# A six-layer local-attention network on one core: the order of every engine's work around the Gelu is rewritten

## The chip, the core and the metric

The kernel runs on one core of a Trainium2 chip. The time is device microseconds of one execution. Before the change the median of three runs is 1857.39 us (1855.83 to 1862.92).

## The reference, cut to what matters

```python
for i in range(6):                                   # DEPTH; x is (8, 256, 128), f32
    x = attn_layer(shift_tokens(x), Wqkv[i], q_scale[i], k_scale[i], Wo[i]) + x
    x = ffn_layer(shift_tokens(x), ln_g[i], ln_b[i], W1[i], b1[i], W2[i], b2[i]) + x

def attn_layer(x, Wqkv, qs, ksc, Wo):                # 16 heads of 64, windows of 32 keys
    q, k, v = split(x @ Wqkv)
    q, k = l2norm(q) * qs, l2norm(k) * ksc           # per token and head
    q, k = q * cos * scale + rotate_half(q) * sin * scale, ...
    sim = where(mask, -max, 8 * q @ k2.T)            # own window and the one before it
    return softmax(sim) @ v2 @ Wo

def ffn_layer(x, g, bln, W1, b1, W2, b2):
    xn = (x - mean) / sqrt(var + 1e-5) * g + bln
    a, gate = split(xn @ W1 + b1)                    # 341 each
    return a * gelu(gate) @ W2 + b2
```

Ahead of the layers come a LayerNorm and a linear attention, and behind them a SiLU gate. The change doesn't touch these.

## The kernel before, in words

The eight batch rows of 256 tokens go through the six layers as 48 steps (`STEPS`), one row and one layer each. A step's work is cut into four units `j` = 0 to 3: an octet of eight heads (`j // 2`) of one tile of 128 tokens (`j % 2`). Each engine has one program, written by hand as a `body(n)` with four slots `j`; steps 3 to 47, 45 of them, run in a hardware loop. In slot `j` of step `n`, with `u = 4n + j`, an engine works on several units at once: the projections and the rotation of unit `u`, the turn (transposition) and the scores of unit `u-2`, the values of unit `u-3`, and pieces of the feed-forward part of steps `n-2` and `n-3`. Every engine runs its own instructions in the order written, and semaphores tie them together.

What the names in the rows are, slot by slot:

- TensorE (PE): `project` writes `ps_q`, `ps_k`, `ps_v`; `turn_qk` writes `ps_qs` and `ps_tk`, and waits for `less_max` of the slot before (`sub_done`), since `ps_qs` held those scores; `turn_p` writes `ps_po`; `scores` needs ScalarE's copies `q_t` and `k_t`; `values` needs ScalarE's copy `p_bd`. `ps_a` is the output projection and the LayerNorm's mean and variance; `ps_f` is shared by `ln_spread`, the three `ff_up` parts and `ff_down`.
- VectorE (DVE): `rotate` (L1076 and L1078, for q and then k), `sum_squares` (L1084, `ssq`), `clamp` (L1094, `ssq_c`), `find_max` (L1116), `less_max` (L1121), `sums` (L1127 and the reciprocal `row_inv`, L1130), and three Newton steps of the inverse norm, `rn_a` (L1099), `rn_b` (L1105) and `rnorm` (L1111). The Newton steps read two tensors in SBUF each, on 128x18 elements. `rotate` of the next slot stands behind all of these.
- ScalarE (ACT): copies out of PSUM (L838), squares (L844), `start_norms` (a logarithm, L876, and an exponential, L878, of 128x18), the softmax's exponential (L944), `ff_copy` (L899, L901) and `gelu` (L906). The Gelu needs another table of functions, and a table load comes ahead of it and one behind it.
- GpSimd (POOL): `divide` (L433, needs `row_inv`), `add_halves` (L418, q and k), `normalise` (L426, q and k, needs `rnorm`), `ff_gate` (L440, L442) in slot 1, `split_slice` (L403, L406) in slot 2, where the layer isn't the last, and `round_x` (L450, L453) in slot 3. Its queue is in the order written as well.

The Gelu of a step stands at the end of ScalarE's slot 0, and its table is changed back in slot 1.

Of the kernel before, what the change touches and what calls it, by code (L numbers as in the profile page):

```python
# [33 lines left out]
QK_SCALE = 8.0  # L34
# [28 lines left out]
def build(nc, x, wq, wk, wv, wp, bp, conv_w, conv_b, wqkv, q_scale, k_scale, wo, ln_g, ln_b, w1, b1, w2,  # L63
          rotary, masks, eye, head_block, out):
    with ExitStack() as ctx:
# [305 lines left out]
        def _(pool):  # L371
# [116 lines left out]
        def _(pe):  # L488
# [281 lines left out]
        def _(act):  # L770
# [83 lines left out]
            def keep_turned(u, j, s):  # L854

                octet, tile = j // 2, j % 2
                wait(act, s_done, u - 1)
                act.wait_ge(tq_done, u + 1)
                copy(q_t[:, s, :], ps_qs[:]).then_inc(q_turned, 1)
                act.wait_ge(tk_done, u + 1)  # L860
# [42 lines left out]

            def gelu(m):
# [13 lines left out]
            def body(n):  # L918
                for j in range(UNITS):
                    u = UNITS * n + j  # L920
                    if live(u - 2):
                        keep_turned(u - 2, (j - 2) % UNITS, j % 2)
                    if live(u):
                        squares_of(u, 0, j % 2)
                    if j == 0 and live(u - 3):
                        keep_p(u - 3, (j - 3) % 2)
                    if live(u):
                        squares_of(u, 1, j % 2)
                    if j > 0 and live(u - 3):
                        keep_p(u - 3, (j - 3) % 2)  # L930
                    if j == 0 and live_batch(n - 2):
                        ln_square(n - 2)
                    if j == 1 and live_batch(n - 3):

                        nc.scalar.preload_act_table_set("natural_log_exp_and_others")
                    if normed(n, j):
                        start_norms(n, j)
                    if j == 0 and live_batch(n - 3):
                        ff_copy(n - 3, 2)
                    if j >= 2 and live_batch(n - 2):  # L940
                        ff_copy(n - 2, j - 2)
                    if live(u - 2):
                        act.wait_ge(sub_done, u - 1)
                        nc.scalar.activation(prob[:, j % 2, :], prob[:, j % 2, :], ACT.Exp,  # L944
                                             scale=QK_SCALE).then_inc(exp_done, 1)
                    if live(u):
                        keep_v(u, n, j)
                    if live(u - 3):
# [357 lines left out]
```

## Time and profile before

| | |
|---|---|
| median of three runs | 1857.39 us |
| profiled execution, own time | 1855.56 us |
| its span | 1853.8 us |
| TensorE busy | 1663.1 us, 90% |
| VectorE, ScalarE, GpSimd busy | 77%, 73%, 70% |
| one steady step | 35.70 us, of which TensorE 33.14 busy |

A busy share is taken over the whole span. TensorE's records are pipelined and their ends are modelled, so starts tell more than ends. In the timelines a row is one or several merged instructions: start in us, time in us, engine, line, operation, output and inputs, and in brackets the idle time of the engine ahead of it with what ended it. The next instruction of VectorE or ScalarE often starts a little before the recorded end of the one ahead.

### The profile page before, as it was taken

How to read it: one execution, taken by the hardware profiler on the slowest of the kernel's cores; microseconds unless marked ns; L12 is line 12 of the kernel's file. 1: busy time of each engine (PE TensorE's matmuls, PEld its weight loads, DVE VectorE, ACT ScalarE, POOL GpSimd, SP SyncE). 2: the span in 40 equal slices, each digit the busy share in tenths (PEclk: the TensorE clock that was granted, in tenths of full speed). 3: DMA queues.
4: the chain of work that ended last, by engine and by line, in shares of the span. 5: the costliest groups of instructions: out<-in, count | busy, mean ns of one | idle time of the engine just before them, and what ended most of it. 6: DMA issues, size and time to landing. Idle time of an engine off the chain costs nothing.

```text
span 1853.8 us, 68588 instructions
## 1 busy us (share of the span) xinstructions
PE 1663.1 (90%) x25968; PEld 1291.5 (70%) x26160; DVE 1430.3 (77%) x3041; ACT 1344.7 (73%) x2656; POOL 1293.3 (70%) x1283
## 2 busy tenths in 40 slices
PE   7889999999999999999999999999999999999973
PEld 5667777777777777677777777767777776777751
DVE  4588878878778787887778778788777777778755
ACT  4267777777777777777777777777777777777753
POOL 5287777777777777777777777777777777677720
PEclk9799999999999999999999999999999999999995
DMA  5011111111101011110111101111110111101000
GB/s 164 11 38 34 32 33 32 30 40 48 32 28 34 28 41 46 33 30 28 34 45 41 34 28 30 31 47 37 33 34 29 33 37 32 30 24 30 25 14 20
DMA packets 41406, 66.13 MB, mean 36 GB/s; under 512 B 7072, under 2 KB 16032, under 8 KB 41376
## 3 DMA queue, kind: packets, MB, share of 16 engines
q1 hardware_dynamic: 40224, 65.38, 11.7%
q10 hardware_dynamic: 1152, 0.34, 0.1%
q8 instruction: 20, 0.33, 0.1%
q14 instruction: 10, 0.08, 0.0%
HBM read 20.61 MB, written 1.05 MB: 12 GB/s over the span
## 4 chain that ended last, share of the span: by engine, by line
PE 68%; ACT 11%; issue 10%; DVE 9%; POOL 1%; ACTq 1%; DMA 0%; DVEq 0%
PE ps_a L490 11%; PE ps_f L490 11%; PE ps_qs L490 9%; PE ps_po L490 8%; PE ps_q L490 7%; PE ps_k L490 5%; PE ps_v L490 5%; PE ps_po L604 4%; PE ps_qs L596 3%; PE ps_tk L596 3%; ACT L906 2%; DVE ssq L1084 2%; DVE prob L1121 2%; ACT p_bd L838 2%; ACT squares L844 2%
## 5 line engine op out<-in xcount | busy, mean ns | idle before, releaser
L426 POOL TENSOR_TENSOR qk<-qk,rnorm 128x512 f32<-128x512 f32 x384 | 393.1, 1045 | 298.2 <-DVE rnorm L1111 298.2
L418 POOL TENSOR_TENSOR qk<-qk,qk_rot 128x512 f32<-128x512 f32 x384 | 483.7, 1276 | 111.1 <-DVE qk_rot L1078 110.8
L1084 DVE TENSOR_REDUCE ssq<-squares 128x8 f32<-128x512 f32 x384 | 257.6, 680 | 71.1 <-ACT squares L844 58.2
L490 PE MATMUL ps_qs<-k_t,q_t 64*32 64x64 f32 x12288 | 210.7, 218 | 67.6 <-ACT k_t L838 46.5
L838 ACT COPY p_bd<-ps_po 64x512 f32<-64x512 f32 x384 | 221.3, 576 | 34.7 <-PE ps_po L604 32.4
L433 POOL TENSOR_TENSOR prob<-prob,row_inv 128x512 f32<-128x512 f32 x192 | 200.3, 1043 | 51.5 <-DVE row_inv L1130 51.5
L1127 DVE TENSOR_REDUCE row_sum<-prob 128x8 f32<-128x512 f32 x192 | 131.7, 686 | 120.6 <-ACT prob L944 120.6
L490 PEld LDWEIGHTS ps_qs<-k_t,q_t 64*32 64x32 f32 x12288 | 179.7, 107 | 57.2 <-issue 57.2
L944 ACT ACTIVATE prob<-prob 128x512 f32<-128x512 f32 x192 | 121.2, 631 | 110.9 <-DVE prob L1121 107.6
L490 PEld LDWEIGHTS ps_po<-p_bd,v_back 128*64 128x64 f32 x3072 | 162.9, 137 | 49.5 <-issue 31.8
L490 PE MATMUL ps_po<-p_bd,v_back 128*64 128x64 f32 x3072 | 193.9, 225 | 1.6 <-ACT p_bd L838 1.5
L490 PE MATMUL ps_po<-p_bd,v_own 128*64 128x64 f32 x3072 | 189.5, 222 | 0.0
L490 PE MATMUL ps_a<-attn_t,wo_sb 128*64 128x257 f32 x1536 | 187.9, 386 | 0.0
L838 ACT COPY k_t<-ps_tk 128x512 f32<-128x512 f32 x192 | 112.9, 588 | 86.7 <-PE ps_tk L596 81.9
L490 PE MATMUL ps_f<-xn,w_sb 128*128 128x256 f32 (+1 forms) x576 | 160.6, 402 | 7.3 <-ACT ff_g L901 1.9
L1076 DVE TENSOR_TENSOR qk<-ps_q,table 128x512 f32<-128x512 f32 x192 | 132.6, 691 | 40.8 <-issue 29.6
L490 PEld LDWEIGHTS ps_po<-p_bd,v_own 128*64 128x64 f32 x3072 | 155.9, 138 | 0.0
L844 ACT ACTIVATE squares<-ps_k 128x512 f32<-128x512 f32 x192 | 115.2, 600 | 54.0 <-DVE qk_rot L1078 52.9
L1076 DVE TENSOR_TENSOR qk<-ps_k,table 128x512 f32<-128x512 f32 x192 | 131.0, 682 | 28.7 <-PE ps_tk L596 28.6
L604 PE MATMUL ps_po<-ident,prob 128*128 128x128 f32 x768 | 119.5, 278 | 31.0 <-POOL prob L433 31.0
L604 PEld LDWEIGHTS ps_po<-ident,prob 128*128 128x128 f32 x768 | 88.1, 140 | 82.5 <-issue 70.0
L844 ACT ACTIVATE squares<-ps_q 128x512 f32<-128x512 f32 x192 | 115.8, 603 | 40.8 <-DVE qk_rot L1078 40.7
(161 smaller groups left out, 4002.6 us busy)
## 6 DMA issues: line engine op xcount, KB each, us to landing
v_back<-v_own SPq DMA_DIRECT2D x192, 192.0 KB, 2.4
w_raw<-in_wqkv SPq DMA_DIRECT2D x48, 192.0 KB, 2.4
v_back<-v_own SPq DMA_DIRECT2D x96, 64.0 KB, 2.1
wo_sb<-in_wo SPq DMA_DIRECT2D x12, 256.0 KB, 3.0
w_sb<-in_w SPq DMA_DIRECT2D x6, 341.0 KB, 3.4
w_sb<-in_w SPq DMA_DIRECT2D x6, 192.0 KB, 2.7
x_in<-in_x SPq DMA_DIRECT2D x4, 256.0 KB, 5.0
out<-s_out SPq DMA_DIRECT2D x8, 128.0 KB, 1.9
```

The source lines that it names most:

```text
L418: nc.gpsimd.tensor_tensor(qk[:, s, i, :], qk[:, s, i, :], qk_rot[:, s, i, :], ALU.add).then_inc(added, 1)
L426: nc.gpsimd.tensor_tensor(heads(qk[:, s, i, :]), heads(qk[:, s, i, :]), rnorm[:, s, 8 * i:8 * i + 8].unsqueeze(2).to_broadcast([P, 8, HEAD ...
L433: nc.gpsimd.tensor_tensor(heads(prob[:, s, :]), heads(prob[:, s, :]), row_inv[:, s, :].unsqueeze(2).to_broadcast([P, 8, HEAD]), ALU.mult). ...
L490: return nc.tensor.matmul(o, lhs, rhs, start=start, stop=stop, **kw)
L596: last = nc.tensor.transpose(ps[:, P * c:P * c + P], qk[:, s, i, P * c:P * c + P], ident[:])
L604: last = nc.tensor.transpose(ps_po[:, P * c:P * c + P], prob[:, s, P * c:P * c + P], ident[:])
L838: return nc.scalar.copy(o, i)
L844: nc.scalar.activation(squares[:, s, OCTET * i:OCTET * i + OCTET], (ps_q, ps_k)[i][:], ACT.Square).then_inc((q_squared, k_squared)[i], 1)
L944: nc.scalar.activation(prob[:, j % 2, :], prob[:, j % 2, :], ACT.Exp, scale=QK_SCALE).then_inc(exp_done, 1)
L1076: V.tensor_tensor(heads(qk[:, s, i, :]), heads(ps[:]), cos.unsqueeze(1).to_broadcast([P, 8, HEAD]), ALU.mult)
L1084: V.tensor_reduce(ssq[:, s, 8 * i:8 * i + 8], heads(squares[:, s, OCTET * i:OCTET * i + OCTET]), AX, ALU.add).then_inc(ssq_done, 1)
L1127: V.tensor_reduce(row_sum[:, s, :], heads(prob[:, s, :]), AX, ALU.add).then_inc(sum_done, 1)
```

## The change: all four engines in another order

No operation is added or taken away; the matrix sizes and the tables stay.

- GpSimd: `normalise` is taken out of the end of its own unit's slot, and stands in the next slot, between `divide` and `add_halves`. `round_x` goes ahead of `add_halves` of slot 3.
- ScalarE: `keep_turned` becomes `keep_queries` and `keep_keys`; the attention copy, now of unit `u-4`, and the `ff_copy` parts stand between them. `gelu` and the last `ff_copy` go from slot 0 to slot 1, behind `keep_keys`. In slot 1, `start_norms` goes behind the exponential and `keep_v`.
- VectorE: in slot 1 `find_max` and `less_max` go ahead of `sum_squares`, and all Newton steps behind `sums`. In slot 2 `ln_normalise` goes behind `find_max`, and `after_ff` to just behind `rotate`.
- TensorE: `ln_spread` goes from early in slot 2 to behind that slot's scores, `ff_up` part 0 behind the values, and `ff_up` part 1 from early in slot 3 to behind `project` of v.

The diff, cut to its core:

```diff
 # GpSimd
                     if live(u - 3):
                         divide(u - 3, (j - 3) % 2)
+                    if live(u - 1):
+                        normalise(u - 1, (j - 1) % 2)
+                    if j == 3 and live(UNITS * (n + 1)):
+                        round_x(n + 1)
                     if live(u):
                         add_halves(u, j % 2)
...
-                    if j == 3 and live(UNITS * (n + 1)):
-                        round_x(n + 1)
-                    if live(u):
-                        normalise(u, j % 2)
 # TensorE
-                        if i == 0 and j == 2 and live_batch(n - 2):
-                            ln_spread(n, n - 2)
-                        if i == 0 and j == 3 and live_batch(n - 2):
-                            ff_up(n - 2, 1)
...
+                    if j == 3 and live_batch(n - 2):
+                        ff_up(n - 2, 1)
                     if live(u - 3):
                         turn_p(u - 3, (j - 3) % 2)
...
                     if j == 2 and live_batch(n - 2):
-                        ff_up(n - 2, 0)
+                        ln_spread(n, n - 2)
...
                     if live(u - 3):
                         values(u - 3, n if j >= 3 else n - 1, (j - 3) % UNITS, (j - 3) % 2)
+                    if j == 2 and live_batch(n - 2):
+                        ff_up(n - 2, 0)
 # ScalarE
-                        keep_turned(u - 2, (j - 2) % UNITS, j % 2)
+                        keep_queries(u - 2, j % 2)
+                    if live(u - 4):
+                        keep_attention(u - 4, n - 1, j)
                     if j == 1 and live_batch(n - 3):
                         ff_copy(n - 3, 2)
+                    if j == 3 and live_batch(n - 2):
+                        ff_copy(n - 2, 0)
                     if live(u - 2):
+                        keep_keys(u - 2, (j - 2) % UNITS)
+
+                    if j == 1:
+                        gelu(n - 3)
+                        keep_p(u - 3, (j - 3) % 2)
+                        squares_of(u, 0, j % 2)
+                        squares_of(u, 1, j % 2)
+                        nc.scalar.preload_act_table_set("natural_log_exp_and_others")
+                        exponential(u - 2, j % 2)
+                        keep_v(u, n, j)
+                        start_norms(n, j)
...
 # VectorE
                         rotate(n, j, 0)
                         rotate(n, j, 1)
                     if j == 0 and live_batch(n - 2):
                         ln_center(n - 2)
                     if j == 2 and live_batch(n - 3):
                         after_ff(n - 3)
+                    if j == 1:
+                        ln_var(n - 2)
+                        find_max(u - 2, j % 2)
+                        less_max(u - 2, j % 2)
+                        sum_squares(u, 0, j % 2)
+                        sum_squares(u, 1, j % 2)
+                        clamp(n, j)
+                        sums(u - 2, j % 2)
+                        newton_1(n, j)
+                        newton_2(n, j)
+                        newton_3(n, j)
...
```

In ScalarE's and VectorE's new branches the `live` tests around the calls are left out here.

VectorE in slot 1 of a loop step, before (rows from the LayerNorm's variance on):

```order
L1145 TENSOR_SCALAR ssq<-ps_a 128x2 [waits var_done]
L1084 TENSOR_REDUCE ssq<-squares 128x8 [waits q_squared]
L1084 TENSOR_REDUCE ssq<-squares 128x8 [waits k_squared]
L1091 ISA
L1094 TENSOR_SCALAR ssq_c<-ssq 128x18 [waits var_ready,ssq_done]
L1116 TENSOR_REDUCE row_max<-ps_qs 128x8 [waits s_done]
L1099 SCALAR_TENSOR_TENSOR rn_a<-ssq_c,rn 128x18 [waits rn_started]
L213 REGISTER_ALU [waits max_done]
L1121 TENSOR_TENSOR prob<-ps_qs,row_max 128x512 [waits pt_done]
L1104 REGISTER_ALU
L1105 TENSOR_TENSOR rn_b<-rn_a,rn 128x18 [waits rn_step]
L1111 SCALAR_TENSOR_TENSOR rnorm<-rn_b,rn 128x18 [waits k_normed,rn_step]
```

The same place in the changed kernel, where lines are numbered 19 higher and the variance row is L1164:

```order
L1135 TENSOR_REDUCE row_max<-ps_qs 128x8 [waits s_done]
L213 REGISTER_ALU [waits max_done]
L1140 TENSOR_TENSOR prob<-ps_qs,row_max 128x512 [waits pt_done]
L1103 TENSOR_REDUCE ssq<-squares 128x8 [waits q_squared]
L1103 TENSOR_REDUCE ssq<-squares 128x8 [waits k_squared]
L1110 ISA
L1113 TENSOR_SCALAR ssq_c<-ssq 128x18 [waits var_ready,ssq_done]
L1146 TENSOR_REDUCE row_sum<-prob 128x8 [waits exp_done]
L1149 RECIPROCAL row_inv<-row_sum 128x8 [waits p_normed,sum_done]
L1118 SCALAR_TENSOR_TENSOR rn_a<-ssq_c,rn 128x18 [waits rn_started]
L1124 TENSOR_TENSOR rn_b<-rn_a,rn 128x18 [waits rn_step]
L1130 SCALAR_TENSOR_TENSOR rnorm<-rn_b,rn 128x18 [waits k_normed,rn_step]
```

The three Newton steps moved from ahead of `row_sum` to behind `row_inv`, which is what releases GpSimd's next `divide`.

ScalarE around the Gelu before, from the end of slot 0 into slot 1:

```order
L838 COPY attn_t<-ps_po 128x4x128 [waits o_done,wo_half_done]
L906 ACT_TABLE_LOAD
L906 ACTIVATE ff_g<-ff_g 128x768 [waits ff1_copied]
L838 COPY q_t<-ps_qs 128x512 [waits tq_done,s_done]
L838 COPY k_t<-ps_tk 128x4x128 [waits tk_done]
L844 ACTIVATE squares<-ps_q 128x512 [waits q_scaled]
L844 ACTIVATE squares<-ps_k 128x512 [waits k_scaled,ssq_done]
L838 COPY p_bd<-ps_po 64x16x32
L935 ACT_TABLE_LOAD
L876 ACTIVATE ssq_ln<-ssq_c 128x18 [waits ssq_clamped]
L878 ACTIVATE rn<-ssq_ln 128x18 [waits ssq_logged]
L944 ACTIVATE prob<-prob 128x512 [waits sub_done]
```

ScalarE at the same place in the changed kernel, slot 1, from the keys' copy on:

```order
L835 COPY k_t<-ps_tk 128x4x128 [waits tk_done]
L910 ACT_TABLE_LOAD
L910 ACTIVATE ff_g<-ff_g 128x768 [waits ff1_copied]
L835 COPY p_bd<-ps_po 64x16x32
L841 ACTIVATE squares<-ps_q 128x512 [waits q_scaled]
L841 ACTIVATE squares<-ps_k 128x512 [waits k_scaled,ssq_done]
L945 ACT_TABLE_LOAD
L906 ACTIVATE prob<-prob 128x512 [waits sub_done]
L835 COPY v_own<-ps_v 128x512 [waits v_done]
L876 ACTIVATE ssq_ln<-ssq_c 128x18 [waits ssq_clamped]
L878 ACTIVATE rn<-ssq_ln 128x18 [waits ssq_logged]
```

The Gelu now stands behind both copies that the scores wait for, and the norms' start behind the exponential.

GpSimd in slots 2 and 3 of the last layer's loop before:

```order
L433 TENSOR_TENSOR prob<-prob,row_inv 128x512
L418 TENSOR_TENSOR qk<-qk,qk_rot 128x512 x2
L426 TENSOR_TENSOR qk<-qk,rnorm 128x512 x2
L433 TENSOR_TENSOR prob<-prob,row_inv 128x512
L418 TENSOR_TENSOR qk<-qk,qk_rot 128x512 x2
L450 COPY xs_hi<-x_run 128x256
L453 TENSOR_TENSOR xs_lo<-x_run,xs_hi 128x256
L426 TENSOR_TENSOR qk<-qk,rnorm 128x512 x2
```

And in the changed kernel:

```order
L433 TENSOR_TENSOR prob<-prob,row_inv 128x512
L426 TENSOR_TENSOR qk<-qk,rnorm 128x512 x2
L418 TENSOR_TENSOR qk<-qk,qk_rot 128x512 x2
L433 TENSOR_TENSOR prob<-prob,row_inv 128x512
L426 TENSOR_TENSOR qk<-qk,rnorm 128x512 x2
L450 COPY xs_hi<-x_run 128x256
L453 TENSOR_TENSOR xs_lo<-x_run,xs_hi 128x256
L418 TENSOR_TENSOR qk<-qk,qk_rot 128x512 x2
```

`qk<-qk,rnorm` moved to the front of a slot, and the additions come last.

## Rows read from the trace of the kernel before

**Rows 1.** The page's first part: busy time of each engine.
```profile
PE 1663.1 (90%) x25968; PEld 1291.5 (70%) x26160; DVE 1430.3 (77%) x3041; ACT 1344.7 (73%) x2656; POOL 1293.3 (70%) x1283
```

**Rows 2.** Timeline of VectorE, one row a step: second and last steady ones.
```profile
207.38 0.41 DVE L1140 TENSOR_TENSOR xc<-x_mid,ps_a 128x256 f32<-128x256 f32 x1
...
1742.43 0.41 DVE L1140 TENSOR_TENSOR xc<-x_mid,ps_a 128x256 f32<-128x256 f32 x1
```

**Rows 3.** Timeline of TensorE, slot 1 of one step.
```profile
924.88 0.66 PE L596 MATMUL ps_qs<-ident,qk 128*128 128x128 f32 x4 [0.28 <-DVE prob L1121]
...
928.38 0.63 PE L604 MATMUL ps_po<-ident,prob 128*128 128x128 f32 x4 [0.57 <-POOL prob L433]
930.01 1.10 PE L490 MATMUL ps_qs<-k_t,q_t 64*32 64x64 f32 x64 [1.00 <-ACT k_t L838]
```

**Rows 4.** Chain of waits, the same slot: start, us, what.
```profile
926.46 0.74 ACT L906
```

**Rows 5.** Timeline of ScalarE, slots 0 and 1 of that step.
```profile
923.95 0.47 ACT L899 ACTIVATE ff_a<-ps_f,b_sb 85x256 f32<-85x256 f32 x1
...
924.85 0.63 ACT L944 ACTIVATE prob<-prob 128x512 f32<-128x512 f32 x1
...
933.15 0.22 ACT L878 ACTIVATE rn<-ssq_ln 128x18 f32<-128x18 f32 x1
934.22 0.63 ACT L944 ACTIVATE prob<-prob 128x512 f32<-128x512 f32 x1 [0.85 <-DVE prob L1121]
934.88 0.58 ACT L838 COPY v_own<-ps_v 128x512 f32<-128x512 f32 x1
```

**Rows 6.** Timeline of VectorE, the same step.
```profile
915.92 0.68 DVE L1121 TENSOR_TENSOR prob<-ps_qs,row_max 128x512 f32<-128x512 f32 x1
...
923.24 0.17 DVE L1094 TENSOR_SCALAR ssq_c<-ssq 128x18 f32<-128x18 f32 x1
...
924.13 0.69 DVE L1121 TENSOR_TENSOR prob<-ps_qs,row_max 128x512 f32<-128x512 f32 x1
...
926.24 0.20 DVE L1130 RECIPROCAL row_inv<-row_sum 128x8 f32<-128x8 f32 x1
...
935.77 0.69 DVE L1076 TENSOR_TENSOR qk<-ps_q,table 128x512 f32<-128x512 f32 x1
...
944.75 0.69 DVE L1076 TENSOR_TENSOR qk<-ps_q,table 128x512 f32<-128x512 f32 x1
...
951.62 0.69 DVE L1121 TENSOR_TENSOR prob<-ps_qs,row_max 128x512 f32<-128x512 f32 x1
```

**Rows 7.** Timeline of GpSimd, the same step.
```profile
925.19 2.04 POOL L426 TENSOR_TENSOR qk<-qk,rnorm 128x512 f32<-128x512 f32 x2 [2.43 <-DVE rnorm L1111]
927.20 1.04 POOL L433 TENSOR_TENSOR prob<-prob,row_inv 128x512 f32<-128x512 f32 x1
928.20 2.50 POOL L418 TENSOR_TENSOR qk<-qk,qk_rot 128x512 f32<-128x512 f32 x2
```

**Rows 8.** Timeline of VectorE, the first steps.
```profile
92.31 0.77 DVE L1094 TENSOR_SCALAR ssq_c<-ssq 128x18 f32<-128x18 f32 x1
...
94.31 0.39 DVE L1105 TENSOR_TENSOR rn_b<-rn_a,rn 128x18 f32<-128x18 f32 x1
...
124.84 0.65 DVE L1099 SCALAR_TENSOR_TENSOR rn_a<-ssq_c,rn 128x18 f32<-128x18 f32 x1
```

**Rows 9.** GpSimd at those times.
```profile
90.54 2.51 POOL L418 TENSOR_TENSOR qk<-qk,qk_rot 128x512 f32<-128x512 f32 x2
...
93.67 0.99 POOL L406 TENSOR_TENSOR w_lo<-w_raw,w_hi 128x384 fp32r<-128x384 f32 x1 [0.18 <-POOL w_hi L403]
...
124.45 1.00 POOL L406 TENSOR_TENSOR w_lo<-w_raw,w_hi 128x384 fp32r<-128x384 f32 x1 [0.18 <-POOL w_hi L403]
```

**Rows 10.** One line over the run: count, ns min/median/max, first and last start.
```profile
L1094 DVE TENSOR_SCALAR ssq_c<-ssq x194: 175/281/767, 72.8 to 1821.0; 128x18 f32<-128x18 f32 x194
```

**Rows 11.** The longest waits: engine line, waited for, us, times, longest.
```profile
POOL qk L426 <- DVE rnorm L1111: 298.2, 191, 2.9
```

More of the change, by code:

```diff
@@ L684, in ln_spread @@
                 wait(pe, ff1_copied, FF_N * m)
+                wait(pe, x_ready, BATCHES + m)
                 for t in range(TILES):
@@ L942, in body @@
                     if live(u - 2):
[L943 to L948, printed above, removed]
-                        keep_attention(u - 3, n if j >= 3 else n - 1, (j - 3) % UNITS)
-                    if j == 0 and live_batch(n - 3):
-                        gelu(n - 3)
+                        keep_keys(u - 2, (j - 2) % UNITS)
@@ new lines, in body @@
+                    if j == 1:
+                        if live_batch(n - 3):
+                            gelu(n - 3)
+                        if live(u - 3):
+                            keep_p(u - 3, (j - 3) % 2)
+                        if live(u):
+                            squares_of(u, 0, j % 2)
+                            squares_of(u, 1, j % 2)
+                        if live_batch(n - 3):
+                            nc.scalar.preload_act_table_set("natural_log_exp_and_others")
+                        if live(u - 2):
+                            exponential(u - 2, j % 2)
+                        if live(u):
+                            keep_v(u, n, j)
+                        if normed(n, j):
+                            start_norms(n, j)
+                    else:
+                        if live(u):
+                            squares_of(u, 0, j % 2)
+                        if j == 0 and live(u - 3):
+                            keep_p(u - 3, (j - 3) % 2)
+                        if live(u):
+                            squares_of(u, 1, j % 2)
+                        if j > 0 and live(u - 3):
+                            keep_p(u - 3, (j - 3) % 2)
+                        if j == 0 and live_batch(n - 2):
+                            ln_square(n - 2)
+                        if normed(n, j):
+                            start_norms(n, j)
+                        if j == 3 and live_batch(n - 2):
+                            ff_copy(n - 2, 1)
+                        if live(u - 2):
+                            exponential(u - 2, j % 2)
+                        if live(u):
+                            keep_v(u, n, j)
@@ L1193, in body @@
                         rotate(n, j, 0)
-                    if j == 2 and live_batch(n - 2):
-                        ln_normalise(n - 2)
-                    if live(u):
                         rotate(n, j, 1)
@@ L1200, in body @@
                         ln_center(n - 2)
-                    if j == 1 and live_batch(n - 2):
-                        ln_var(n - 2)
-                    if live(u):
-                        sum_squares(u, 0, j % 2)
-                        sum_squares(u, 1, j % 2)
-                    if normed(n, j):
-                        clamp(n, j)
                     if j == 2 and live_batch(n - 3):
                         after_ff(n - 3)
-                    if live(u - 2):
-                        find_max(u - 2, j % 2)
@@ L1225, in body @@
-                    if live(u - 2):
-                        sums(u - 2, j % 2)
+                    if j == 1:
+                        if live_batch(n - 2):
+                            ln_var(n - 2)
+                        if live(u - 2):
+                            find_max(u - 2, j % 2)
+                            less_max(u - 2, j % 2)
+                        if live(u):
+                            sum_squares(u, 0, j % 2)
+                            sum_squares(u, 1, j % 2)
+                        if normed(n, j):
+                            clamp(n, j)
+                        if live(u - 2):
+                            sums(u - 2, j % 2)
+                        if normed(n, j):
+                            newton_1(n, j)
+                            newton_2(n, j)
+                            newton_3(n, j)
+                    else:
+                        if live(u):
+                            sum_squares(u, 0, j % 2)
+                            sum_squares(u, 1, j % 2)
+                            clamp(n, j)
+                        if live(u - 2):
+                            find_max(u - 2, j % 2)
+                        if j == 2 and live_batch(n - 2):
+                            ln_normalise(n - 2)
+                        if live(u):
+                            newton_1(n, j)
+                        if j == 3 and live(u):
+                            newton_2(n, j)
+                            newton_3(n, j)
+                        if j == 3 and live_batch(n - 1):
+                            after_attention(n - 1)
+                        if live(u - 2):
+                            less_max(u - 2, j % 2)
+                        if j != 3 and live(u):
+                            newton_2(n, j)
+                            newton_3(n, j)
+                        if live(u - 2):
+                            sums(u - 2, j % 2)
```

42 lines of the change are left out of this document (7 added, 35 removed).

## The prediction, made before the changed kernel ran

> **What bounds the kernel now.** I read the page's busy shares first: TensorE 90%, VectorE 77%, ScalarE 73%, GpSimd 70% [rows 1]. Then the length of a step: 43 steps lie between the two marks of VectorE, (1742.43 - 207.38) / 43 = 35.70 us [rows 2]. 45 looped steps make 1606 of the 1853.8 us, so what counts is the time of one step. Third, TensorE's timeline: it idles almost only in slot 1, 0.28 us for `less_max`, 0.57 for `divide`, 1.00 for the keys' copy, 1.85 together [rows 3]. Fourth, the chain of waits: in slot 1 it leaves TensorE and runs through the Gelu on ScalarE [rows 4]. The rest of the step is TensorE's.
>
> So the step is a loop of nearly balanced engines, and I cut it at three marks of VectorE [rows 6]: A, from slot 3's `less_max` (915.92) to slot 0's (924.13), 8.21 us; B, from there to the start of slot 2's `rotate` (935.77), 11.64; C, from there to slot 3's next `less_max` (951.62), 15.85. The sum is 35.70. A and B run on VectorE and ScalarE, C partly on TensorE. For each I ask what the new order makes of it.
>
> **What the trace shows of VectorE beside GpSimd.** `clamp` takes 175 ns at least, 281 at the median and 767 at most [rows 10], with the same 128x18 elements every time. The 0.77 us one began at 92.31 and ended at 93.08 [rows 8]; GpSimd's two additions ran from 90.54 to 93.05 [rows 9]. The free one of 923.24 took 0.17 [rows 6]. A Newton step is held alike: `rn_b` at 94.31 took 0.39 and ended at 94.70, `rn_a` at 124.84 took 0.65 and ended at 125.49 [rows 8]; GpSimd's `w_lo` ended at 94.66 and 125.45 [rows 9]. So `clamp` and the Newton steps end 0.03 to 0.04 us behind the GpSimd instruction that runs when they start. Before the change GpSimd mostly waits while the Newton steps run, because `normalise` waits for their result: 298.2 us in 191 waits [rows 11]. The change takes this wait away, and so puts GpSimd at work exactly then.
>
> The rule behind this is in the Trainium skill, "SBUF — State Buffer", section "Who interferes with whom": a VectorE instruction with two SBUF inputs, or in a two-port mode, and a GpSimd instruction shut each other out for whole instructions, and the one that issues first decides. It speaks against this change. The trace agrees (0.65 us against 0.17 to 0.18 for the same form).
>
> **The change, stretch by stretch.**
>
> A. The order on VectorE and ScalarE in slot 0 stays, apart from copies that have slack. GpSimd's queue after `row_inv` is now `divide` 1.00 (927.20 to 928.20, start to start), `normalise` 2.01 (925.19 to 927.20), the additions 2.5 [rows 7]. They start 0.1 behind the reciprocal's end and are over 5.6 behind it. The reciprocal ends 2.3 behind `less_max` (924.13 to 926.24 + 0.20), so in front of slot 0 at about 918.2 (915.92 + 2.3), and `clamp` stands at 923.24 [rows 6], 5.0 behind it: it is held until 923.85, and `find_max` and `less_max` behind it start 0.46 later. A = 8.67. TensorE's wait for that `less_max` grows with it.
>
> B. ScalarE is busy from the exponential's start in slot 0 (924.85) to the end of `start_norms` in slot 1 (933.15 + 0.22 = 933.37), 8.52 us [rows 5]. The new queue adds the last `ff_copy`, 0.90 (923.95 to 924.85), and, ahead of `start_norms`, the exponential and `keep_v`, 1.2 (0.63 + 0.58) [rows 5], less 0.1 for the overlap of neighbours: 10.5 in all, with no idle time. From `less_max` to the exponential is 0.72 (924.13 to 924.85), so the Newton steps can begin 11.25 behind `less_max`. Three of them and the way to `rotate` are 0.6: 11.85, which is 0.2 later than now, though TensorE gets its scores and values about 1.3 us sooner. And they are held: `row_inv` ends at nearly the same time as the norms' start, and `divide`, 1.04 long [rows 7], is released by it 0.09 later, when only `rn_a` has been issued. `rn_b` then waits for the end of `divide`: one more microsecond. B = 12.85. If `rn_a` comes second, it is held instead, at the same price.
>
> C. In slot 2 the four rotations, `after_ff` and two sums bring `clamp` to 4.25 behind `rotate`; GpSimd's additions run to 4.6 and hold it 0.4. Then `find_max`, `ln_normalise`, and `rn_a`, which meets `w_lo` of `split_slice` (1 us long [rows 9]) and loses 0.7 of it; `less_max` comes at 6.3, so slot 3's `rotate` starts 8.66 behind slot 2's (now 944.75 - 935.77 = 8.98 [rows 6], since the exponential there no longer stands behind the first `ff_copy`). In slot 3 now 6.87 pass to `less_max` (951.62 - 944.75). In the new order `round_x` is over only 4.2 after `rotate`, and the two additions follow at once, to 6.75. `rn_a` waits for the first of them, `rn_b` for the second, and `after_attention` and `less_max` stand behind: 7.33. C = 8.66 + 7.33 = 16.0.
>
> What lies beside: `ff_up` part 1 waits some 0.3 us for its `ff_copy` in slot 3, `values` of slot 2 some 0.5 for `p_bd`; both are inside C, hidden by VectorE being later still. `round_x` waits for `project` of v of its own slot, which is done before GpSimd comes to it. The moved `ff_down`, `ln_spread` and DMA issues cost nothing beyond this; if VectorE were not late, the two waits would give 0.3 of the gain back.
>
> **Sum.** 8.67 + 12.85 + 16.0 = 37.5 against 35.70: +1.8 us a step, times 45 = +82. The eight steps of the last layer have no `split_slice`, -0.65 each, -5. That is +77 on the profiled execution's own 1855.6: 1933. (It lies 1.8 below the median of the three runs.) Of unknown price is only how far a held engine slips in between: from below nothing (each step runs on as if alone) to a whole GpSimd instruction of 1.0 to 1.28 for every Newton step, which in slots 1 and 3 would be some 1.1 more a step, 1933 + 50 = 1983. I take one instruction lost in slot 1 and two in slot 3, because `rn_b` at 94.31 waited behind a `w_lo` that had begun at 93.67 [rows 9], between the Newton step ahead of it and itself.
>
> **The rivals.**
>
> 1. VectorE runs its Newton steps through before GpSimd gets in, in one of the two slots. Slot 3 free: C = 15.25 (then TensorE sets it), 36.8 a step, 1855.6 + 48 = 1904. Slot 1 free: 36.5, 1892. For it: the gaps between the three steps are 0.03 us. Against: `rn_b` above.
>
> 2. Only `clamp` is held, the Newton steps never: 8.67 + 11.85 + 15.25 = 35.77, 1859, no change. Against it stands `rn_a` at 124.84. The Trainium skill's page "Advanced Engine Details and Errata", section "VectorE Performance Modes", names only two-port instructions as shut out by GpSimd, and would give this; the 0.65 us of `rn_a`, an instruction with two inputs, disagrees with it.
>
> 3. The other side: nothing is held much, because the semaphores place GpSimd elsewhere than I reckon. Then A = 8.21, B = 11.85 and C = 14.9 (TensorE from slot 2's `ff_up` on), 34.95 a step, -0.75 x 45 = -34: 1822. It decides if `clamp` and `rn_a` stay under 0.2 us in slots 0 and 1. For it: the scores leave the Gelu's shadow for certain. Against: the 43 identical steps and the sums above, all tied to `row_inv`.
>
> 4. The change does all it can: the 1.85 us of slot 1 go, 45 x 1.85 = 83, 1772. Against: the first 0.28 waits for a `less_max` that no edit brings forward, and ScalarE's queue of 10.5 us in B is longer than before.
>
> **How the numbers follow.** Forecast (1915 to 1960) 0.56; rival 1 (1875 to 1915) 0.17; rival 2 0.07; rival 3 0.12; rival 4 0.05; worse than 1960 0.03. The likeliest is 1933, its own range 1905 to 1960. The range of 8 in 10 takes in rivals 1 and 2 and leaves out 3, 4 and the worst: 1850 to 1960. A measurement here tells 0.5% (9 us) from no change; faster by more has rivals 3 and 4, 0.17; within it 0.08; slower by more 0.75.
>
> **What would show it.** A step of 37.5 us on VectorE's `xc`; GpSimd's wait for `rnorm` nearly gone; `clamp` in slot 0 at about 0.6 us, `rn_b` in slot 1 at about 0.9 and in slot 3 over 1; the Gelu behind `k_t` and the scores of slot 1 starting within 1 us of the turn; TensorE idle instead at slot 1's first turn, about 1 us, and in slots 2 and 3; its busy share near 86%. Wrong I am if `rn_b` keeps its 0.17 everywhere, or if a step is under 35.7.

## The result, and the profile after

The changed kernel takes 1927.17 us, the median of four runs (1920.98 to 1933.91); the kernel before takes 1859.52 in its four beside them. The ratio is 1.0365, 95% interval 1.0322 to 1.0408: 3.7% slower. The forecast was 1933, in a range of 1850 to 1960. The profiled execution took 1920.98 us of its own time, against the 1855.56 from which the sum was made: +65.4.

The page's busy times, and the shares of the chain that ended last:

```profile
PE 1727.4 (90%) x26160; PEld 1283.6 (67%) x26160; DVE 1595.5 (83%) x3041; ACT 1326.9 (69%) x2655; POOL 1287.6 (67%) x1283
...
DVE 47%; ACT 25%; issue 18%; PE 6%; DVEq 2%; POOL 1%; ACTq 1%; DMA 0%; POOLq 0%
```

The chain's shares before the change:

```profile
PE 68%; ACT 11%; issue 10%; DVE 9%; POOL 1%; ACTq 1%; DMA 0%; DVEq 0%
```

Two readings. VectorE is busy for 165 us more than in [rows 1] (1595.5 - 1430.3), with the same 3041 instructions: they became longer. And the chain is VectorE's for 47% and TensorE's for 6%, where before it was TensorE's for 68% and VectorE's for 9%. TensorE's own share says 90% in both: it can't tell the two cases apart. The chain's shares alone prove little either: in e4 below, whose step is as long, 46% of it is GpSimd's.

Which instructions became longer, shows the view by line and shape (the last two numbers are busy us, mean ns of one):

```profile
L1113 DVE TENSOR_SCALAR ssq_c<-ssq 128x18 f32<-128x18 f32 x194 | 120.6, 622 | 6.7
L1124 DVE TENSOR_TENSOR rn_b<-rn_a,rn 128x18 f32<-128x18 f32 x194 | 112.7, 581 | 3.4
L1118 DVE SCALAR_TENSOR_TENSOR rn_a<-ssq_c,rn 128x18 f32<-128x18 f32 x194 | 80.1, 413 | 1.6 <-ACT rn L878 1.6
L1130 DVE SCALAR_TENSOR_TENSOR rnorm<-rn_b,rn 128x18 f32<-128x18 f32 x194 | 36.7, 189 | 6.7
```

Together these four small ones (the clamp and the three Newton steps) take 350.1 us. The same view of the kernel before gives them as:

```profile
L1094 DVE TENSOR_SCALAR ssq_c<-ssq 128x18 f32<-128x18 f32 x194 | 69.0, 356 | 6.7
L1099 DVE SCALAR_TENSOR_TENSOR rn_a<-ssq_c,rn 128x18 f32<-128x18 f32 x194 | 42.5, 219 | 39.8 <-ACT rn L878 39.8
L1111 DVE SCALAR_TENSOR_TENSOR rnorm<-rn_b,rn 128x18 f32<-128x18 f32 x194 | 34.5, 178 | 6.6
L1105 DVE TENSOR_TENSOR rn_b<-rn_a,rn 128x18 f32<-128x18 f32 x194 | 33.2, 171 | 1.8
```

That is 179.2, so 170.9 us more: all of VectorE's growth. `ssq_c` is the clamp; its median was 281 ns [rows 10] and is 609 now.

Where in a step they are held, shows VectorE's timeline. Answering to [rows 6], one step from slot 0's clamp on:

```profile
922.20 0.41 DVE L1159 TENSOR_TENSOR xc<-x_mid,ps_a 128x256 f32<-128x256 f32 x1
...
924.15 0.63 DVE L1113 TENSOR_SCALAR ssq_c<-ssq 128x18 f32<-128x18 f32 x1
...
925.50 0.69 DVE L1140 TENSOR_TENSOR prob<-ps_qs,row_max 128x512 f32<-128x512 f32 x1
...
936.52 0.20 DVE L1149 RECIPROCAL row_inv<-row_sum 128x8 f32<-128x8 f32 x1
936.64 0.18 DVE L1118 SCALAR_TENSOR_TENSOR rn_a<-ssq_c,rn 128x18 f32<-128x18 f32 x1
936.86 1.03 DVE L1124 TENSOR_TENSOR rn_b<-rn_a,rn 128x18 f32<-128x18 f32 x1
...
938.09 0.69 DVE L1095 TENSOR_TENSOR qk<-ps_q,table 128x512 f32<-128x512 f32 x1
...
942.12 0.60 DVE L1113 TENSOR_SCALAR ssq_c<-ssq 128x18 f32<-128x18 f32 x1
...
943.62 0.79 DVE L1118 SCALAR_TENSOR_TENSOR rn_a<-ssq_c,rn 128x18 f32<-128x18 f32 x1
...
950.54 0.52 DVE L1113 TENSOR_SCALAR ssq_c<-ssq 128x18 f32<-128x18 f32 x1
...
951.59 0.69 DVE L1118 SCALAR_TENSOR_TENSOR rn_a<-ssq_c,rn 128x18 f32<-128x18 f32 x1
952.32 1.19 DVE L1124 TENSOR_TENSOR rn_b<-rn_a,rn 128x18 f32<-128x18 f32 x1
...
954.23 0.69 DVE L1140 TENSOR_TENSOR prob<-ps_qs,row_max 128x512 f32<-128x512 f32 x1
...
959.60 0.41 DVE L1159 TENSOR_TENSOR xc<-x_mid,ps_a 128x256 f32<-128x256 f32 x1
```

And GpSimd's, answering to [rows 7]:

```profile
922.23 2.53 POOL L418 TENSOR_TENSOR qk<-qk,qk_rot 128x512 f32<-128x512 f32 x2
...
936.81 1.04 POOL L433 TENSOR_TENSOR prob<-prob,row_inv 128x512 f32<-128x512 f32 x1 [1.49 <-DVE row_inv L1149]
938.18 2.05 POOL L426 TENSOR_TENSOR qk<-qk,rnorm 128x512 f32<-128x512 f32 x2 [0.33 <-DVE rnorm L1130]
...
950.98 2.50 POOL L418 TENSOR_TENSOR qk<-qk,qk_rot 128x512 f32<-128x512 f32 x2
```

Put the ends side by side. The clamp ends at 924.78, the additions at 924.76. `rn_b` of slot 1 ends at 937.89, `divide` at 937.85. In slot 3 `rn_a` ends at 952.28 and `rn_b` at 953.51; the two additions, a pair from 950.98 to 953.48, meet at about 952.2. Each held instruction ends 0.02 to 0.05 us behind the GpSimd instruction that ran when it started.

TensorE's timeline of that step, its idle times from 0.2 us on, answers to [rows 3]:

```profile
926.25 0.66 PE L596 MATMUL ps_qs<-ident,qk 128*128 128x128 f32 x4 [0.97 <-DVE prob L1140]
...
940.96 0.71 PE L490 MATMUL ps_f<-ident,rnorm 128*128 128x128 f32 x4 [0.32 <-DVE x_run L1178]
...
942.37 0.34 PE L490 MATMUL ps_po<-p_bd,v_back 128*64 128x64 f32 x4 [0.70 <-ACT p_bd L835]
...
943.88 1.13 PE L490 MATMUL ps_f<-xn,w_sb 128*128 128x256 f32 x4 [0.36 <-DVE xn L1172]
...
955.05 0.65 PE L596 MATMUL ps_qs<-ident,qk 128*128 128x128 f32 x4 [0.20 <-DVE prob L1140]
```

The waits of [rows 3] for `divide` (0.57) and for the keys' copy (1.00) are gone, as the reordering intends. The one for `less_max` grew from 0.28 to 0.97, and three new ones stand in slot 2.

The step is 959.60 - 922.20 = 37.40 us, against 35.70 [rows 2]. The steps of this kernel take 37.28 and 37.4 us by turns up to the last layer, 37.34 on average; this is one of the longer. By the prediction's three stretches:

| stretch | before | forecast | after |
|---|---|---|---|
| A | 8.21 | 8.67 | 8.67 |
| B | 11.64 | 12.85 | 12.59 |
| C | 15.85 | 16.0 | 16.14 |
| step | 35.70 | 37.5 | 37.40 |

### The profile page after: what moved, and what is told of

Same layout as the page of the kernel before. It is cut to its first block, busy times and chain, and to the rows that moved or that the text cites. A ratio compares the mean times of both kernels' runs of the same rounds, so it can differ in the third digit from the quotient of the medians.

```text
span 1919.1 us, 68780 instructions
## 1 busy us (share of the span) xinstructions
PE 1727.4 (90%) x26160; PEld 1283.6 (67%) x26160; DVE 1595.5 (83%) x3041; ACT 1326.9 (69%) x2655; POOL 1287.6 (67%) x1283
## 4 chain that ended last, share of the span: by engine, by line
DVE 47%; ACT 25%; issue 18%; PE 6%; DVEq 2%; POOL 1%; ACTq 1%; DMA 0%; POOLq 0%
DVE qk_rot L1097 6%; DVE ssq L1103 6%; ACT squares L841 6%; DVE rn_b L1124 5%; DVE row_sum L1146 5%; DVE prob L1140 5%; DVE row_max L1135 4%; ACT p_bd L835 4%; ACT prob L906 4%; DVE qk L1095 4%; DVE rn_a L1118 3%; DVE ssq_c L1113 3%; ACT L945 3%; ACT attn_t L835 2%; PE ps_f L490 2%
## 5 line engine op out<-in xcount | busy, mean ns | idle before, releaser
L426 POOL TENSOR_TENSOR qk<-qk,rnorm 128x512 f32<-128x512 f32 x384 | 393.2, 1046 | 16.2 <-DVE rnorm L1130 15.9
L1103 DVE TENSOR_REDUCE ssq<-squares 128x8 f32<-128x512 f32 x384 | 253.2, 681 | 51.3 <-ACT squares L841 47.7
L490 PE MATMUL ps_f<-xn,w_sb 128*128 128x256 f32 (+1 forms) x576 | 163.6, 407 | 25.0 <-DVE xn L1172 16.8
L596 PE MATMUL ps_qs<-ident,qk 128*128 128x128 f32 x768 | 120.1, 279 | 59.7 <-DVE prob L1140 57.7
L1135 DVE TENSOR_REDUCE row_max<-ps_qs 128x8 f32<-128x512 f32 x192 | 131.3, 684 | 39.9 <-PE ps_qs L490 39.6
L596 PEld LDWEIGHTS ps_qs<-ident,qk 128*128 128x128 f32 x768 | 88.1, 140 | 112.5 <-DVE prob L1140 74.5
L490 PEld LDWEIGHTS ps_f<-xn,w_sb 128*128 128x128 f32 (+1 forms) x576 | 92.1, 179 | 69.1 <-ACT ff_g L901 30.1
```

Of the source, the lines that this page charges most:

```text
L426: nc.gpsimd.tensor_tensor(heads(qk[:, s, i, :]), heads(qk[:, s, i, :]), rnorm[:, s, 8 * i:8 * i + 8].unsqueeze(2).to_broadcast([P, 8, HEAD ...
L490: return nc.tensor.matmul(o, lhs, rhs, start=start, stop=stop, **kw)
L596: last = nc.tensor.transpose(ps[:, P * c:P * c + P], qk[:, s, i, P * c:P * c + P], ident[:])
L1103: V.tensor_reduce(ssq[:, s, 8 * i:8 * i + 8], heads(squares[:, s, OCTET * i:OCTET * i + OCTET]), AX, ALU.add).then_inc(ssq_done, 1)
L1135: V.tensor_reduce(row_max[:, s, :], heads(ps_qs[:]), AX, ALU.max).then_inc(max_done, 1)
```

## The experiments

The theory is: with nothing held the new order is a gain, and the held clamp and Newton steps turn it into a loss. The rivals are that the new order itself is slow (its queues on ScalarE and TensorE), or that GpSimd's part alone is. Each ratio below is to the kernel before, run beside it; steps are measured from `xc` to `xc` as above. The medians of before were 1861.09, 1860.22 and 1859.67 us in the three sets of runs.

### e1: the changed kernel, nothing that can be held

```diff
-  V.tensor_scalar(ssq_c[:, s, :], ssq[:, s, :], 1e-24, SQ_SCALE, ALU.max, ALU.mult)
+  V.tensor_reduce(ssq_c[:, s, :], ssq[:, s, :].unsqueeze(2), AX, ALU.add)
+  nc.scalar.activation(ssq_ln, ssq_c, ACT.Ln, scale=SQ_SCALE)
-  newton_1, newton_2, newton_3: two SBUF inputs each
+  V.tensor_reduce(rn_a, rn_0.unsqueeze(2), AX, ALU.add)      # the same for rn_b, rnorm
```

> The changed kernel with the same four small VectorE instructions a slot (clamp and the three Newton steps), at the same places and with the same waits, but each written as a one-input reduction over an axis of length one. This leaves out the clamp and the Newton refinement of the inverse norms (the scale goes into the logarithm), so that none of the four has a second SBUF input or a two-port form. Theory (held by GpSimd's instructions): every one of them takes under 0.25 us again, A falls from 8.67 to 8.2, B from 12.6 to 11.75, C from 16.1 to about 15.2, the step from 37.40 to about 35.1 us, the time from 1921 to about 1825. Rival (the new order of the queues itself is what costs, above all ScalarE's longer run in slot 1, and the holds fill slack): the step stays above 37 us and the time above 1905.

Measured: 1811.03 us, ratio 0.9731 (0.9705 to 0.9757). The step is 34.93: A 8.20, B 11.73, C 15.01. The 194 clamps and 194 `rn_b` of the run (count, then ns at least, median, at most):

```profile
L1113 DVE TENSOR_REDUCE ssq_c<-ssq x194: 160/172/174, 73.1 to 1779.9; 128x18 f32<-128x18 f32 x194
...
L1123 DVE TENSOR_REDUCE rn_b<-rn_a x194: 158/171/174, 74.0 to 1780.8; 128x18 f32<-128x18 f32 x194
```

No instance is above 0.174 us, at the same places beside the same GpSimd instructions. TensorE's waits of the step shrink to two:

```profile
943.75 0.66 PE L596 MATMUL ps_qs<-ident,qk 128*128 128x128 f32 x4 [0.28 <-DVE prob L1138]
...
959.01 0.34 PE L490 MATMUL ps_po<-p_bd,v_back 128*64 128x64 f32 x4 [0.23 <-ACT p_bd L835]
```

So all the holds together cost 37.40 - 34.93 = 2.47 us a step, and the order without them is faster than before. The rival of slow queues falls.

### e2: only the Newton steps can't be held

The edit is e1's for the Newton steps alone:

```diff
   V.tensor_scalar(ssq_c[:, s, :], ssq[:, s, :], 1e-24, SQ_SCALE, ALU.max, ALU.mult)   # stays
+  V.tensor_reduce(rn_a, rn_0.unsqueeze(2), AX, ALU.add)      # the same for rn_b, rnorm
```

> As the first, but the clamp keeps its real two-port form; only the three Newton steps are one-input reductions (this leaves out the refinement). Theory: clamp stays at about 0.6 us in slots 0 and 2, A stays 8.67, B is 11.75, C about 15.3 to 15.5, the step about 35.8 us and the time about 1855. If only the clamp mattered: the step stays at 37.4. Rival (order of queues): above 37 us.

Measured: 1879.20 us, ratio 1.0103 (1.0084 to 1.0122), step 36.31: A 8.65 and B 11.72 as expected, C 15.94 where 15.3 to 15.5 were expected. That was a miss. The holds of the Newton steps went, and the clamp, which comes earlier now, met the additions instead. VectorE's clamps of slots 0 to 3:

```profile
900.68 0.63 DVE L1113 TENSOR_SCALAR ssq_c<-ssq 128x18 f32<-128x18 f32 x1
...
911.21 0.67 DVE L1113 TENSOR_SCALAR ssq_c<-ssq 128x18 f32<-128x18 f32 x1
...
917.79 1.10 DVE L1113 TENSOR_SCALAR ssq_c<-ssq 128x18 f32<-128x18 f32 x1
...
926.54 1.27 DVE L1113 TENSOR_SCALAR ssq_c<-ssq 128x18 f32<-128x18 f32 x1
```

In slots 2 and 3 of the changed kernel they took 0.60 and 0.52. A sum over holds can't be taken apart: who is freed from one runs into the next.

### e3 and e10: the kernel before, nothing that can be held

```diff
   # the kernel before
-  tensor_scalar for the clamp, newton_1, newton_2, newton_3
+  e3: the four reductions of e1;  e10: the four of e5 (below), which keep the whole computation
```

> The kernel before with the same replacement of clamp and Newton steps by one-input reductions (leaves out clamp and refinement). Theory: it had few holds (clamp 0.3 to 0.4 us in slots 1 to 3, rn_a 0.1 to 0.2 in slot 3), some of them beside slack: the step falls from 35.70 to between 35.2 and 35.6 us, the time to 1830 to 1850. The difference to the first kernel then is what the new order alone does. Rival: no difference, 35.70.

> The kernel before with only the clamp and Newton steps as one-input reductions, the whole computation kept. By the theory that its holds lie beside slack the step stays at 35.7 us and the time within 0.3% of before; the reductions are some 0.1 us longer in all than the plain copies tried before, so up to 35.8. If the reductions alone were what makes the changed kernel with them fast, this would come to 35.1, 1822 to 1830.

Measured: e3 1855.37 us, ratio 0.9978 (0.9955 to 1.0002), step 35.71. e10 1861.73 us, ratio 1.0022 (1.0007 to 1.0037), step 35.84. Before, the four instructions were held for some 40 us over the run (179.2 less 194 x 4 x 0.177), and taking that away gives nothing that can be measured: there they lie beside VectorE's slack, where TensorE and ScalarE set the time. In slot 1, for example, the clamp is held for 0.38 us before, and `rn_a` then waits 0.84 for ScalarE; in e3 nothing is held, and that wait is 1.22. e3's expectation of a small gain was a miss. With e1 it prices the order alone: 35.71 to 34.93, -0.78 a step.

### e4: the kernel before with GpSimd's part of the change alone

```diff
                     if live(u - 3):
                         divide(u - 3, (j - 3) % 2)
+                    if live(u - 1):
+                        normalise(u - 1, (j - 1) % 2)
+                    if j == 3 and live(UNITS * (n + 1)):
+                        round_x(n + 1)
                     # add_halves, ff_gate, split_slice; normalise(u) and round_x are gone from here
```

> The kernel before with the GpSimd part of the change alone: normalise a slot later, ahead of the additions, and round_x ahead of them; all other engines as before. Theory: clamp is held in slots 0, 1 and 2, a Newton step by ff_gate in slot 1 and by w_lo in slot 2; A 8.67, B about 12.0, C about 16.8, the step about 37.5 us and the time 1930 to 1945. Rival (order of the other engines is what costs): GpSimd no longer makes TensorE wait for divide, so the step is 35.7 or less and the time at most 1857.

Measured: 1939.27 us, ratio 1.0428 (1.0408 to 1.0447), step 37.47: A 8.66, B 12.04, C 16.77, against 8.67, 12.0 and 16.8 expected. GpSimd's part alone makes the whole loss and more; the other engines' new order takes 0.07 of it back. The lengths came as forecast, the places not quite: in slot 2 the clamp ran free (0.18), and in slot 3 it was held instead. Two of VectorE's held ones, in slots 2 and 3:

```profile
947.54 0.74 DVE L1105 TENSOR_TENSOR rn_b<-rn_a,rn 128x18 f32<-128x18 f32 x1
...
954.53 0.99 DVE L1094 TENSOR_SCALAR ssq_c<-ssq 128x18 f32<-128x18 f32 x1
```

### e7: the changed kernel with GpSimd's old order

```diff
-                    if live(u - 1):
-                        normalise(u - 1, (j - 1) % 2)
                     # add_halves, ff_gate, split_slice; round_x behind them again
+                    if live(u):
+                        normalise(u, j % 2)
```

> The changed kernel with GpSimd's order as before the change; the new orders of VectorE, ScalarE and TensorE stay. Theory: the Newton steps run free (GpSimd waits for rnorm), A is 8.2, B 11.85; but divide stands behind a normalise that is due later in slot 1, so TensorE's turn of slot 2 waits for it; the step about 35.8 us, within 0.3 of the 35.70 of before, the time about 1858. Rival (the other engines' order is what costs): 36.5 or more.

Measured: 1883.30 us, ratio 1.0131 (1.0110 to 1.0153), step 36.40: A 8.21 and B 11.73 free of holds, C 16.46. Another miss: without GpSimd's part the rest is not a gain but a loss of 0.7 a step. TensorE and GpSimd in slots 1 and 2 show why:

```profile
946.90 0.63 PE L604 MATMUL ps_po<-ident,prob 128*128 128x128 f32 x4 [0.57 <-POOL prob L433]
...
957.66 0.63 PE L604 MATMUL ps_po<-ident,prob 128*128 128x128 f32 x4 [1.45 <-POOL prob L433]
```

```profile
954.46 2.05 POOL L426 TENSOR_TENSOR qk<-qk,rnorm 128x512 f32<-128x512 f32 x2 [3.32 <-DVE rnorm L1130]
956.47 1.04 POOL L433 TENSOR_TENSOR prob<-prob,row_inv 128x512 f32<-128x512 f32 x1
```

The Newton steps of slot 1 stand behind the sums now, so `normalise` of that unit waits 3.32 us for them at the end of GpSimd's slot, and `divide`, ready long before, is queued behind it. The same stretch has a hold too: in slot 2 `rn_a` takes 0.85 us, right ahead of `less_max`. No run parts the two, so how much of the loss is the late `divide` stays open. So the two parts need each other: GpSimd's costs 1.77 without the rest (e4) and the rest costs 0.70 without GpSimd's (e7), while both without holds gain 0.78 (e1).

### e6: the reciprocal of slot 1 behind the Newton steps

```diff
-                            sums(u - 2, j % 2)            # row_sum and row_inv
+                            sums(u - 2, j % 2, True)      # row_sum alone
                         newton_1, newton_2, newton_3
+                            inverse(u - 2, j % 2)         # row_inv
```

> The changed kernel with one instruction moved: in slot 1 VectorE's reciprocal (row_inv), which releases GpSimd's divide, stands behind the three Newton steps instead of ahead of them. Theory: rn_b in slot 1 falls from 1.03 to 0.17 us, B from 12.59 to about 11.8; part of it is given back, since divide and all of GpSimd behind it in slot 2 come 1.3 us later; the step 36.4 to 36.9 us, the time 1877 to 1900. Rival (divide's lateness costs TensorE as much, or the hold filled slack): no change, 37.4.

Measured: 1876.23 us, ratio 1.0082 (1.0052 to 1.0111), step 36.30: A 8.66, B 11.85, C 15.79. In slot 1 GpSimd has nothing to start on until the Newton steps are over, and `rn_b` took 0.18. B loses 0.74, as forecast for it. C fell by 0.35 against the changed kernel, which I had not expected, so step and time came out just under the lower edge of the expectation. The trace shows where. GpSimd comes later in slot 2 as well, so the clamp and `rn_a` there take 0.38 and 0.33 in place of 0.60 and 0.79, and `less_max` comes 0.68 sooner behind `rotate`. Then `rnorm` is held in their stead:

```profile
932.51 0.99 DVE L1130 SCALAR_TENSOR_TENSOR rnorm<-rn_b,rn 128x18 f32<-128x18 f32 x1
```

It stands behind `less_max`, where VectorE of the changed kernel waits 0.40 for the exponential before `row_sum`, and so costs 0.34 and not 0.81. B isolates the slot 1 hold, and shows that the place of the reciprocal, just ahead of the Newton steps or behind them, decides it.

### e5: the whole computation, written so that nothing is held

```diff
-  V.tensor_scalar(ssq_c, ssq, 1e-24, SQ_SCALE, ALU.max, ALU.mult)
+  V.tensor_reduce(fac[..., 1], ssq_f, AX, ALU.max)           # ssq beside a constant 1e-24
-  nc.scalar.activation(rn_0, ssq_ln, ACT.Exp, scale=-0.5)
+  nc.scalar.activation(fac[..., 2:5], ssq_ln (three times), ACT.Exp, scale=-0.5)
-  newton_1, newton_2, newton_3
+  V.tensor_reduce(sum3[..., 0], fac[..., 0:4], AX, ALU.mult) # -0.5 * scale * x * r * r
+  V.tensor_reduce(fac[..., 5], sum3, AX, ALU.add)            # + 1.5
+  V.tensor_reduce(rnorm, fac[..., 4:6], AX, ALU.mult)        # * r
```

The factors of each norm lie side by side, so one input carries them all. The logarithm takes the scale factor.

> The changed kernel with the whole computation kept: clamp and Newton steps as one-input reductions over small side-by-side factors (a maximum with 1e-24, a product of four, a sum with 1.5, a product of two). None has a second SBUF input or a two-port form. Theory: as the first kernel, none of them over 0.3 us, A 8.2, B 11.8, C 15.0, the step 34.9 to 35.1 us, the time 1808 to 1822, 2 to 2.7% under the kernel before. Rival (what helped there was that the refinement was left out): the time is above 1850.

Measured: 1820.11 us, ratio 0.9791 (0.9770 to 0.9811), step 35.13: A 8.25, B 11.86, C 15.03. The reductions take 0.19, 0.23, 0.19 and 0.19 us, at most 0.231, and none is held. With every operation kept the changed order is 2.1% faster than the kernel before.

### e8 and e9: no operation rewritten, only GpSimd's order mixed

```diff
                     divide(u - 3, (j - 3) % 2)
-                    if live(u - 1):
+                    if j in (1, 2) and live(u - 1):
                         normalise(u - 1, (j - 1) % 2)
-                    (round_x of slot 3)
                     # add_halves, ff_gate, split_slice
+                    (round_x of slot 3)
+                    if j in (2, 3) and live(u):
+                        normalise(u, j % 2)
```

with e6's edit. Units 0 and 1 are normalised a slot later, units 2 and 3 at the end of their own. In slot 3 GpSimd then waits 0.54 us for the norms, as before; in slot 2 its `w_lo` still runs while they are made. e9 is e8 with e5's reductions.

> An order made by the theory alone, with every instruction in its own form: GpSimd normalises units 0 and 1 in the next slot, as changed, units 2 and 3 at the end of their own slot, as before, and round_x stands behind the additions; VectorE's reciprocal of slot 1 stands behind the Newton steps. Theory: no hold in slot 0 (A 8.2), none on a Newton step in slots 1 and 3, clamp held 0.3 us in slot 2: B 11.8, C 15.5, the step about 35.4 us, the time 1840 to 1850. Rival: 35.7 or more.

> The mixed order (normalise of units 0 and 1 in the next slot, of 2 and 3 at the end of their own, round_x behind the additions, the reciprocal of slot 1 behind the Newton steps) with the clamp and the Newton steps as one-input reductions, the whole computation kept. If holds are all that the GpSimd order costs, this order has nothing to save any more and the step is that of the changed kernel with the same reductions: 35.13 us, 1820 us, between 35.0 and 35.2. If the mixed order is better in itself (GpSimd's queue no longer late for something), it is 34.9 or less, under 1812. If the normalisation at the end of slots 2 and 3 costs something of its own (divide behind it, as with GpSimd's old order), it is 35.3 to 35.6, 1828 to 1845. VectorE's share of busy time falls from 82% to 77% either way.

Measured: e8 1828.47 us, ratio 0.9839 (0.9821 to 0.9858), step 35.25: A 8.22, B 11.83, C 15.20. e9 1826.80 us, ratio 0.9820 (0.9804 to 0.9837), step 35.22: B 11.95, C 15.03. So an order worked out from where the holds fall gets 1.6% with the original instructions. In e9 nothing is left to save, and the mixed order gains nothing over e5's; its 35.22 lies at the upper edge of "the same" and under "a cost of its own". The medians, 6.7 us apart, point to a small cost of its own, but they are from different sets of runs, and I leave it open. Some of the four small instructions in e8, in slots 0, 1, 2 and 3:

```profile
914.15 0.18 DVE L1115 TENSOR_SCALAR ssq_c<-ssq 128x18 f32<-128x18 f32 x1
...
926.40 0.18 DVE L1126 TENSOR_TENSOR rn_b<-rn_a,rn 128x18 f32<-128x18 f32 x1
...
933.24 0.99 DVE L1132 SCALAR_TENSOR_TENSOR rnorm<-rn_b,rn 128x18 f32<-128x18 f32 x1
...
938.96 0.89 DVE L1115 TENSOR_SCALAR ssq_c<-ssq 128x18 f32<-128x18 f32 x1
...
940.39 0.63 DVE L1120 SCALAR_TENSOR_TENSOR rn_a<-ssq_c,rn 128x18 f32<-128x18 f32 x1
941.05 0.18 DVE L1126 TENSOR_TENSOR rn_b<-rn_a,rn 128x18 f32<-128x18 f32 x1
```

The long holds of `rn_b` in slots 1 and 3 are gone. Many others remain, and not all of them were foreseen: besides the rows above the clamp of slot 1 takes 0.69. The four together take 258.7 us over the run, some 120 more than free ones and three times what the kernel before loses. Yet its step is 35.25, against 35.22 in e9, which has none. The forecast of 1840 to 1850 missed on the good side: it had C at 15.5 with fewer holds than there are, and 15.20 was measured.

## Why the prediction was right, step by step

- **A: 8.67 forecast, 8.67 measured.** The clamp takes 0.63 in place of 0.17. Everything in it (the reciprocal's 2.3, the queue of 5.6, the clamp at 5.0) came out to 0.1 us. e1 takes the hold away, and A is 8.20.
- **B: 12.85 forecast, 12.59 measured.** ScalarE's queue from the exponential of slot 0 to the norms' start was put at 10.5 us and took 10.4 (926.22 to 936.61). `divide` starts 0.09 behind the reciprocal's end and gets in ahead of `rn_b`, as reckoned; the hold of 0.86 (1.03 less 0.17) was taken at 1.0, and the Newton steps began 11.14 behind `less_max`, not 11.25. e6 and e1 give 11.85 and 11.73 without it.
- **C: 16.0 forecast, 16.14 measured.** In slot 2 the clamp lost 0.42 (0.60 in all) and `rn_a` 0.61 (0.79), where 0.4 and 0.7 were forecast, and slot 3's `rotate` came 8.52 behind slot 2's (8.66). Slot 3 took 7.62 where 7.33 stood: the additions ended 6.87 behind `rotate`, not 6.75, and from there to `less_max` 0.75 passed, not 0.58. Its clamp was held too, 0.34 (0.52 in all), which I had not counted; but `rn_a` behind it waits for the end of the first addition either way, so that hold doesn't lengthen the slot. The wait of `values` named beside it was 0.70 and not 0.5; that VectorE covers it was not tested by itself. What TensorE would set without VectorE's delay, 14.9, was 15.01 in e1.
- **The choice of how a held engine slips in.** One instruction lost in slot 1, two in slot 3: both so (1.03; 0.69 and 1.19). This was the estimate with the widest bounds, and luck had a part in it. The row of the kernel before that it rested on (`rn_b` at 94.31 behind a `w_lo` that began at 93.67, [rows 8, 9]) is another case: there `less_max` stood between the two Newton steps, so it did not show what happens to two steps 0.04 us apart. Rival 1 needed one slot to be free, and none was. The row of that `less_max`, before the change:

```profile
93.71 0.69 DVE L1121 TENSOR_TENSOR prob<-ps_qs,row_max 128x512 f32<-128x512 f32 x1
```

- **Rival 2, only the clamp is held,** falls by `rn_b` at 1.03 and 1.19 us. Both forms are told apart in e2 as well: with the clamp alone left to be held, A keeps its 8.65, and B loses its hold. The Trainium skill's page "Advanced Engine Details and Errata", section "VectorE Performance Modes", names only two-port instructions, and these rows show that the section is too narrow. The Trainium skill's page "SBUF — State Buffer", section "Who interferes with whom", names those with two SBUF inputs as well, and the trace agrees. That section also says that a reduction never contends on this chip; e1's 0.174 us at most agrees.
- **Rival 3, nothing is held,** had the price right: 34.95 a step and 1822 against e1's 34.93 and 1811, and e5's 35.13 and 1820. Its place was in a kernel without the holds.
- **Rival 4** falls with e1: with no hold at all the gain is 0.78 a step, not 1.85. ScalarE's longer queue keeps B at 11.73, above the 11.64 of before.
- **The sum.** 1.8 a step was 1.70 in the step shown and 1.64 on average, and the last layer's steps gave 0.4 back, not 0.65. Over the 43 steps between the marks that is +67.5 us (from 1535.05 to 1602.57); the sum's 1.8 x 43 - 5 makes 72. The ends were counted as two more steps, +3.6, and measured -2.2 (+5.5 ahead of the first mark, -7.7 behind the last). Hence 1933 against the execution's own 1920.98; the median, 1927.17, is nearer.
- **What I said would show it.** GpSimd's wait for `rnorm` is down from 298.2 us [rows 11] to 15.9. The busy share near 86% was wrong: it is 90% (94 to 95% in e1, e5 and e8). Recorded ends of TensorE are modelled and some records were missing before (25,968 in place of 26,160), so a share of it was no test.

Of the experiments' own expectations those of e2, e3, e7 and e8 missed, and e6's by a little. e3, e6 and e8 show why a hold's price depends on where it lies; e2 and e7 why no part can be priced with the others left out.

## What to carry to other kernels

Before you give an idle engine work to do, look at what runs on its neighbour in that idle time: here GpSimd's wait of 1.6 us a slot was what let VectorE's Newton steps run in 0.17 us each. The sign is one instruction of one size with a minimum, median and maximum far apart (175, 281, 767 ns), whose ends coincide with another engine's. The cure is either the order of two or three instructions (e8) or a form with one input (e5), and its worth is that of the place on the path, not of the time held (e3, e8).

## What the runs showed of the hardware

- Between two Newton steps 0.04 us apart on VectorE, GpSimd's next instruction got in, in slots 1 and 3 of the step shown. In slot 3 `rn_a` is held for the first addition and `rn_b` for the second (0.69 and 1.19 us). The additions themselves take 2.50 us there, no longer than before [rows 7].
- A one-input reduction over 128x18 outputs (0.16 to 0.23 us) was never held in 194 instances of each kind. It can multiply, add or take a maximum over up to four factors that lie side by side. The reciprocal on 128x8 wasn't held either (202 to 206 ns over 192 instances before the change), with GpSimd at work beside it: that of 926.24 [rows 6] ran within the `normalise` from 925.19 to 927.23 [rows 7]. In the changed kernel GpSimd is idle at that point, waiting for it, so its 202 to 205 ns there say nothing.
- A held instruction is recorded as busy, not as idle: VectorE's share rose from 77% to 83% with no work added, and fell to 76% in e1.
